# Four-layer graph stack: the layer normalisation moved from ScalarE to VectorE, its maximum taken in a later eviction, and ScalarE's order of work changed

## The reference, cut to what matters

```
h = max(layernorm(x), 0); x = x + gru_gnn(h, adj)       # layer 0: 5 message steps with a GRU cell
h = max(layernorm(x), 0); x = x + gated_gnn(h, adj)     # layer 1: gate, homophilic and heterophilic part, elu
h = max(layernorm(x), 0); x = x + grouped_gcn(h, adj)   # layer 2: 5 groups among nodes 0..24, two convolutions each
h = max(layernorm(x), 0); x = x + gcn(h, adj)           # layer 3
layernorm(x) = (x - mean) / sqrt(var + 1e-5), over the 128 features
```

## Time and profile before

| | us |
|---|---|
| median of 3 runs | 786.51 (783.95 to 788.78) |
| profiled execution | 786.21 |
| its span, first to last instruction | 784.4 |
| PE busy | 691.5 (88%) |
| DVE busy | 599.7 (76%) |
| ACT busy | 521.8 (67%) |
| POOL busy | 298.6 (38%) |

### The profile page before, as it was taken

One profiled execution on the slowest core, in us unless ns is written; L12 is line 12 of the kernel. 1 busy time (PEld: TensorE's weight loads), 2 busy tenths in 40 slices (PEclk: granted clock), 3 DMA queues, 4 the chain that ended last, 5 costly groups with the idle time before them and its releaser, 6 DMA issues.

```text
span 784.4 us, 12359 instructions
## 1 busy us (share of the span) xinstructions
PE 691.5 (88%) x4091; PEld 583.5 (74%) x4091; DVE 599.7 (76%) x1461; ACT 521.8 (67%) x1083; POOL 298.6 (38%) x423
## 2 busy tenths in 40 slices
PE   3899899989999979989999989989999989975765
PEld 2678588878888768878888767878788867865544
DVE  4688997888978966888978977888976877876143
ACT  5566677578778766668768757767767656646533
POOL 4222424573334343363343343463332242453320
PEclk9999989999999999999999999999999999999769
DMA  6600011100000020300000020210000000200001
GB/s 152 167 26 1 2 35 25 51 2 4 8 1 1 1 57 21 116 28 3 7 3 1 1 57 10 72 28 4 6 3 1 1 1 1 80 28 7 5 1 55
DMA packets 47623, 21.08 MB, mean 27 GB/s; under 512 B 9032, under 2 KB 47560, under 8 KB 47560
## 3 DMA queue, kind: packets, MB, share of 16 engines
q1 hardware_dynamic: 47560, 20.29, 9.6%
HBM read 15.27 MB, written 4.19 MB: 25 GB/s over the span
## 4 chain that ended last, share of the span: by engine, by line
PE 43%; DVE 30%; ACT 13%; POOL 8%; issue 5%; DMA 1%; DVEq 0%; SPq 0%; POOLq 0%; ACTq 0%
PE bank L404 7%; PE bank L405 7%; PE bank L406 6%; PE bank L399 5%; DVE zd L1292 4%; DVE hd L1304 4%; DVE h L1296 4%; DVE bank L1318 3%; DVE rh L1315 3%; POOL rstd L908 2%; PE bank L593 2%; ACT bank L880 2%; ACT xn L689 2%; PE bank L528 2%; DVE h_hi L1299 2%
## 5 line engine op out<-in xcount | busy, mean ns | idle before, releaser
L924 POOL TENSOR_TENSOR h_lo<-h,h_hi 128x512 fp32r<-128x512 f32 x64 | 81.8, 1279 | 339.8 <-DVE h_hi L1299 339.8
L404 PE MATMUL bank<-h_hi,whh_hi 128*128 128x512 f32 x240 | 106.7, 445 | 13.3 <-DVE rh L1315 12.8
L1315 DVE SCALAR_TENSOR_TENSOR rh<-bank,rh 128x512 f32<-128x512 f32 x80 | 55.0, 687 | 68.6 <-ACT bank L874 68.6
L404 PE MATMUL bank<-g_hi,wc_hi 128*128 128x512 f32 x240 | 103.6, 432 | 0.7 <-DVE h L1296 0.3
L406 PE MATMUL bank<-h_lo,whh_hi 128*128 128x512 f32 x240 | 96.3, 401 | 0.0
L405 PE MATMUL bank<-h_hi,whh_lo 128*128 128x512 f32 x240 | 96.1, 401 | 0.0
L405 PE MATMUL bank<-g_hi,wc_lo 128*128 128x512 f32 x240 | 94.9, 395 | 0.0
L406 PE MATMUL bank<-g_lo,wc_hi 128*128 128x512 f32 x240 | 94.8, 395 | 0.0
L399 PEld LDWEIGHTS bank<-edge,hn 128*128 128x128 f32 x640 | 83.6, 191 | 8.2 <-issue 1.0
L689 ACT ACTIVATE xn<-x_res,shift,rstd 128x128 f32<-128x128 f32 x128 | 55.8, 485 | 48.7 <-POOL shift L910 48.7
L399 PE MATMUL bank<-edge,hn 128*128 128x128 f32 x640 | 84.3, 274 | 0.8 <-ACT hn L859 0.8
(11 more groups left out here) (167 smaller groups left out, 1605.9 us busy)
## 6 DMA issues: line engine op xcount, KB each, us to landing
x_in<-in_x SPq DMA_DIRECT2D x8, 512.0 KB, 5.4
adj_in<-in_adj SPq DMA_DIRECT2D x8, 512.0 KB, 4.8
x_res<-in_x SPq DMA_DIRECT2D x16, 256.0 KB, 2.8
out_x<-x_res SPq DMA_DIRECT2D x16, 256.0 KB, 2.3
xz<-x_res SPq DMA_DIRECT2D x16, 50.0 KB
w_sb<-in_L_gnn_W SPq DMA_DIRECT2D x1, 640.0 KB, 5.1
w_sb<-in_L_gnn_W SPq DMA_DIRECT2D x5, 128.0 KB, 5.0
rows<-in_adj SPq DMA_DIRECT2D x32, 0.6 KB
```

The costliest lines, as they stand in the source:

```text
L404: nc.tensor.matmul(dst[:], w_hi, m_hi, start=start, stop=False)
L924: nc.gpsimd.tensor_tensor(h_lo[q][:], h[q][:], h_hi[q][:].bitcast(f32), ALU.subtract).then_inc(sem["h_lo_new"], 1)
L1315: nc.vector.scalar_tensor_tensor(rh[:], R_BANK[:], 1.0, rh[:], ALU.add, ALU.mult).then_inc(sem["rh_ready"], 1)
```

## The change

- **Normalisation.** ACT's `norm_relu` and `zone_norm` go. DVE gets `norm`, four `tensor_scalar` a quad, (x - mean) * rstd, both read per partition from tiles, at NORM1, NORM3 and NORM0, all four graphs in the first of the two slots, and `zone_norm` at NORM2. POOL's -mean and shift go, with one wait.
- **Maximum.** It is taken where the transpose is evicted (`first_h`, `read_zone`, `read_last_norm`: Copy becomes Relu). In layer 1, where xn is multiplied untransposed too, ACT does it in place, `second_norm`, one 128x512 activation a quad at NORM1 + 1 (slots -1, 1, 3, 5).
- **Second support.** `read_support2` moves from DVE to ACT, ahead of `read_hidden`.
- **Order on ACT.** `beside(2n+1)` no longer comes before the next step's eviction of H_BANK but behind it, ahead of `turned_h`; only `l1_read_linear` stays at the end of the step. `read_blocks` moves ahead of `second_norm`.
- **DVE's slots.** `make_bias_rows` goes from slot 20 to slot 8; the second half of `group_blocks` from slot 23 to slot 24.

The diff, with the declarations of tiles and semaphores left out:

```diff
...
 TURN_ADJ, DEGREES_ABS, DEGREES, GROUP_DEGREES, GROUP_BLOCKS, TURN_BLOCKS = 22, 12, 17, 20, 22, (27, 29)
-DEGREE_NORMS, ADD_IDENTITY, MASK_ROUND, LAST_NORMS, BIAS_ROWS = 26, 31, 34, 38, 24
+BIAS_AT = 8
+DEGREE_NORMS, ADD_IDENTITY, MASK_ROUND, LAST_NORMS = 26, 31, 34, 38
 STATS0, AGGR0, NORM0, TURN0, EDGES, SPLIT = 13, 14, 16, 26, 33, 35
...
         def _(act):
-            def norm_relu(L, r, q, src, dst, graphs=range(QUAD)):
-                i = 0 if L == 0 else 1
-                if graphs[0] == 0:
-                    act.wait_ge(sem[f"ln{L}_rstd"], r * QUADS + q + 1)
-                for j in graphs:
-                    b = q * QUAD + j
-                    last = nc.scalar.activation(dst[:, b, :], src[:, b, :], ACT.Relu,
-                                                bias=shift[i][:, b:b + 1], scale=rstd[i][:, b:b + 1])
-                if graphs[-1] == QUAD - 1:
-                    last.then_inc(sem[f"ln{L}_xn"], 1)
+            def second_norm(r, q):
+                act.wait_ge(sem["l1_centred"], r * QUADS + q + 1)
+                nc.scalar.activation(xn[:, cols(q), :], xn[:, cols(q), :], ACT.Relu).then_inc(sem["ln1_xn"], 1)
...
                     act.wait_ge(sem["h_new"], (r - 1) * STEPS + q + 1)
-                nc.scalar.activation(hx[q][:], (C_BANK if r else (A_BANK, B_BANK)[q % 2])[:], ACT.Copy
+                nc.scalar.activation(hx[q][:], (C_BANK if r else (A_BANK, B_BANK)[q % 2])[:], ACT.Relu
                                      ).then_inc(sem["hx_ready"], 1)
...
-            for q in range(QUADS):
-                norm_relu(0, 0, q, x_in, x_in)
             for q in range(QUADS):
...
-            def zone_norm(r, q):
-                act.wait_ge(sem["ln2_rstd"], r * QUADS + q + 1)
-                nc.scalar.activation(xz[0:PACKED, q, :], xz[0:PACKED, q, :], ACT.Relu,
-                                     bias=shift[2][0:PACKED, q:q + 1], scale=rstd[2][0:PACKED, q:q + 1]
-                                     ).then_inc(sem["ln2_xn"], 1)
             def read_zone(r, q):
                 act.wait_ge(sem["zone_turned"], r * QUADS + q + 1)
-                nc.scalar.activation(zone[:, q, :], H_BANK[:, 0:PACKED], ACT.Copy).then_inc(sem["zone_ready"], 1)
+                nc.scalar.activation(zone[:, q, :], H_BANK[:, 0:PACKED], ACT.Relu).then_inc(sem["zone_ready"], 1)
...
+            def read_support2(r, k):
+                n = TILES[k][3]
+                act.wait_ge(sem["l2_sup2"], r * NT + k + 1)
+                nc.scalar.activation(sup2[0:n, k % 2, :], C_BANK[0:n, 0:128], ACT.Copy).then_inc(sem["l2_sup2_read"], 1)
             def read_group(r, k, at):
...
                 act.wait_ge(sem["ln3_turned"], r * QUADS + q + 1)
-                nc.scalar.activation(hT[q % 2][:], quad(A_BANK[:, :]), ACT.Copy).then_inc(sem["ln3_h"], 1)
+                nc.scalar.activation(hT[q % 2][:], quad(A_BANK[:, :]), ACT.Relu).then_inc(sem["ln3_h"], 1)
...
                     l1_read_turned(r, q)
-                for r, q in due(slot, 1, LINEAR1):
-                    l1_read_linear(r, q)
                 for r, k, _ in second_conv(slot)[-1:]:
...
                     read_group(r, k, at)
+                for r, k in tile_at(slot, 2):
+                    read_support2(r, k)
                 for r, k in tile_at(slot, 1):
...
                     l1_exp(r, q)
-                for r, q in due(slot, 1, NORM2):
-                    zone_norm(r, q)
                 for r, _ in due(slot, 1, PACK_EARLY, units=1):
...
                 for half in range(2):
-                    for r, q in due(slot, 1, NORM1 + half):
-                        norm_relu(1, r, q, x_res, xn, range(2 * half, 2 * half + 2))
-                    for r, q in due(slot, 1, NORM3 + half):
-                        norm_relu(3, r, q, x_res, xn, range(2 * half, 2 * half + 2))
-                    for r, q in due(slot, -1, NORM0 + half):
-                        norm_relu(0, r, q, x_in, x_in, range(2 * half, 2 * half + 2))
+                    for r, _ in due(slot, 0, TURN_BLOCKS[half], units=1):
+                        read_blocks(r, half)
+                for r, q in due(slot, 1, NORM1 + 1):
+                    second_norm(r, q)
                 for r, q in due(slot, 0, TURN_ADJ, pace=1):
...
                     first_h(r, q)
-                for half in range(2):
-                    for r, _ in due(slot, 0, TURN_BLOCKS[half], units=1):
-                        read_blocks(r, half)
...
                 nc.scalar.activation(g_hi[:], TG[:], ACT.Copy).then_inc(sem["g_hi_ready"], 1)
+            def linear_beside(slot):
+                for r, q in due(slot, 1, LINEAR1):
+                    l1_read_linear(r, q)
...
                 nc.scalar.activation(rh[:], H_BANK[:], ACT.Identity, bias=bhh[:, 2:3]).then_inc(sem["hb_ready"], 1)
+                beside(2 * n - 1)
                 if n + 1 < ALL:
...
                 nc.scalar.activation(I_BANK[:], I_BANK[:], ACT.Tanh, bias=bih[:, 2:3]).then_inc(sem["n_ready"], 1)
-                beside(2 * n + 1)
+                linear_beside(2 * n + 1)
             for n in range(ALL, ALL + TAIL_STEPS):
+                beside(2 * n - 1)
                 beside(2 * n)
-                beside(2 * n + 1)
+                linear_beside(2 * n + 1)
+            beside(2 * (ALL + TAIL_STEPS) - 1)
...
             nc.gpsimd.memset(neg_half[:], -0.5)
-            nc.gpsimd.memset(neg_one[:], -1.0)
             nc.gpsimd.memset(eps_ln[:], LN_EPS)
...
                 pool.wait_ge(sem[f"ln{L}_mv"], r * QUADS + q + 1)
-                nc.gpsimd.tensor_tensor(var_eps[i][0:p, c], mv[i][0:p, c, 1], eps_ln[0:p, c], ALU.add)
-                nc.gpsimd.tensor_tensor(neg_mean[i][0:p, c], mv[i][0:p, c, 0], neg_one[0:p, c], ALU.mult).then_inc(sem[f"ln{L}_var"], 1)
+                nc.gpsimd.tensor_tensor(var_eps[i][0:p, c], mv[i][0:p, c, 1], eps_ln[0:p, c], ALU.add).then_inc(sem[f"ln{L}_var"], 1)
                 pool.wait_ge(sem[f"ln{L}_var"], r * QUADS + q + 1)
-                nc.gpsimd.tensor_tensor(rstd[i][0:p, c], var_eps[i][0:p, c], neg_half[0:p, c], ALU.pow).then_inc(sem[f"ln{L}_pow"], 1)
-                pool.wait_ge(sem[f"ln{L}_pow"], r * QUADS + q + 1)
-                nc.gpsimd.tensor_tensor(shift[i][0:p, c], neg_mean[i][0:p, c], rstd[i][0:p, c], ALU.mult).then_inc(sem[f"ln{L}_rstd"], 1)
+                nc.gpsimd.tensor_tensor(rstd[i][0:p, c], var_eps[i][0:p, c], neg_half[0:p, c], ALU.pow).then_inc(sem[f"ln{L}_rstd"], 1)
...
+            def norm(L, r, q, src, dst, done):
+                i = 0 if L == 0 else 1
+                dve.wait_ge(sem[f"ln{L}_rstd"], r * QUADS + q + 1)
+                for j in range(QUAD):
+                    b = q * QUAD + j
+                    last = nc.vector.tensor_scalar(dst[:, b, :], src[:, b, :], mv[i][:, b, 0:1], rstd[i][:, b:b + 1],
+                                                   ALU.subtract, ALU.mult)
+                last.then_inc(sem[done], 1)
+            def zone_norm(r, q):
+                dve.wait_ge(sem["ln2_rstd"], r * QUADS + q + 1)
+                nc.vector.tensor_scalar(xz[0:PACKED, q, :], xz[0:PACKED, q, :], mv[2][0:PACKED, q, 0:1],
+                                        rstd[2][0:PACKED, q:q + 1], ALU.subtract, ALU.mult).then_inc(sem["ln2_xn"], 1)
             def edges(r, q):
...
                 mean_variance(0, 0, q)
+            for q in range(QUADS):
+                norm(0, 0, q, x_in, x_in, "ln0_xn")
             dve.wait_ge(sem["weights_loaded"], 16 * N_EARLY)
...
-            def read_support2(r, k):
-                n = TILES[k][3]
-                dve.wait_ge(sem["l2_sup2"], r * NT + k + 1)
-                nc.vector.tensor_copy(sup2[0:n, k % 2, :], C_BANK[0:n, 0:128]).then_inc(sem["l2_sup2_read"], 1)
             def add_group(r, k):
...
                     mean_variance(1, r, q)
+                for r, q in due(slot, 1, NORM1):
+                    norm(1, r, q, x_res, xn, "l1_centred")
+                for r, q in due(slot, 1, NORM3):
+                    norm(3, r, q, x_res, xn, "ln3_xn")
+                for r, q in due(slot, -1, NORM0):
+                    norm(0, r, q, x_in, x_in, "ln0_xn")
+                for r, q in due(slot, 1, NORM2):
+                    zone_norm(r, q)
                 for r, q in due(slot, 1, STATS2):
...
                     l1_gate(r, q)
-                for r, k in tile_at(slot, 2):
-                    read_support2(r, k)
                 for r, k, _ in second_conv(slot):
...
                     degrees(r, q)
-                if slot == BIAS_ROWS - 4:
+                if slot == BIAS_AT:
                     make_bias_rows()
...
                     group_degrees(r)
-                for r, half in due(slot, 0, GROUP_BLOCKS, pace=1, units=2):
+                for r, half in due(slot, 0, GROUP_BLOCKS, pace=2, units=2):
                     if half == 0:
...
```

(9 more changed lines are left out.)

## The result

The kernel after takes 820.85 us (median of 4 runs, 818.99 to 822.00) against 785.37 us before on the same chip: ratio 1.0399, 95% interval 1.0359 to 1.0440. The forecast was 776.2. The sign was wrong.

The account below looks back on a forecast made before the run. PE was taken as the bound in most slots, DVE close, with ACT's in-order queue carrying POOL's delay into PE in slots 26 to 31. Three rounds -10.8, first round +2.3, start and tail -1.5: 786.2 becomes 776.2 us, range 760 to 793.

Parts of the forecast that it names:

- Slots 26 to 31 (-5.5 a round): Three rounds: ACT no longer delays the norm, rh and PE's turn come earlier, eviction waits go; -5.5 us a round, bounds -8, -2.
- the eviction's wait (3.2 a round): Slots 26 to 31: PE's wait for H_BANK's eviction, 9.5 us over 11 waits, 3.2 a round, all goes.
- rival B: The eviction's wait only changes its name, as ACT's moved work stands ahead of turned_h: 791.5 us; chance 0.17.
- Slot 32 (+2.2): Fourth quad's norm on DVE is held by four POOL operations ahead of rh: +2.2 us a round, bounds 0 and +3.6.
- Slot 38 and slots 0 to 6 (+1.8 and +1.2): NORM1's first quad held by POOL, +1.8 us a round; ACT's fuller queue in slots 4 and 6 and DVE's order, +1.2.
- Slots 8 to 25 (-3.3): PE's waits for eviction and second support go, layer 0's norm costs about 0.3: -3.3 us a round, bounds -4, +2.
- Four instructions in 0.65 us: DVE's price for one quad's four norm tensor_scalar in a row: 0.65 us, between 0.45 and 1.1.
- First round (+2.3): DVE-bound slots 16 to 23 take four norms, bias rows move from slot 20 to 8: +2.3 us, bounds -1.5, +5.
- Start and tail (-1.5): Shorter instructions at the start, a shorter first norm of layer 3 in the tail: -1.5 us together, bounds -5, +2.
- A: Collisions of DVE's norms with POOL cost nothing, as short instructions slip in between: 762.4 us; chance 0.26.
- C: DVE becomes the bound in slots 36 to 2 and 16 to 22, norms held at nearly every quad: 807 us; chance 0.13.
- slots 26 to 31 no shorter than 30 us a round: Sign named ahead that the forecast is wrong: slots 26 to 31 still take 30 us a round or more.

Follow-up runs that it names:

- e3: The kernel after with VectorE's norms of layers 1, 3 and 0 listed behind the other work of their slot: 802.80 us, ratio 1.0164.
- e1: The kernel before with only two ScalarE parts: H_BANK's eviction ahead of the work beside, second support copied by ScalarE: 785.23 us, ratio 0.9958.
- e2: The kernel after with ScalarE's old order and the second support copied by VectorE again: 824.70 us, ratio 1.0442.
- e5: e3's kernel with GpSimd's add_identity in slots 32 and 38 waiting until the norm beside it is done: 787.09 us, ratio 0.9971.
- e14: Zone's norm added on VectorE to a kernel with the ScalarE parts and only layer 3's norm there (757.66 us): 764.33 us, ratio 0.9680.
- e13: Layer 0's norm of rounds 1 to 3 added on VectorE to a kernel with ScalarE's parts and only layer 3's norm there (757.66 us): 770.09 us, ratio 0.9751.

## Why the forecast was wrong, by its own steps

- **Slots 26 to 31 (-5.5 a round)** is the step that failed. With slot 32 it holds 22 of the 46 us between the forecast and the trace; 11 lie in start and tail, 10 in slots 8 to 25. The step let four norm instructions end 0.65 us after rstd and rh follow. The listing of `beside` puts the norms ahead of zone_residual and its statistics, so rstd is waited for with nothing in between (2.36 us), and 1.11 + 0.67 + 0.87 us come behind it before rh. With slot 32 the forecast had -3.3; measured were +2.9, +3.7 and +5.9. e3 moves nothing but this order and gives 18 us back.
- In the same step, **the eviction's wait (3.2 a round)** was counted as won. e1 shows that it isn't: PE's wait at L562 goes, and the steps of slots 24 to 34 stay as long. After against e2 says the same with the norm on VectorE. That rh sets their length instead is a reading: PE's wait for rh rose from 12.8 to 16.9 us in e1. This was rival B's case, in these slots alone, and not by B's mechanism, which wanted a new wait of PE there.
- **Slot 32 (+2.2)**: the collision is there, but it takes 3.5 a round (e5), near the upper bound of 3.6. The forecast gave 2 us of slack away because rh had been idle 2.83 us; that idle time was itself the wait for ScalarE, and the change had removed it (in e3 VectorE waits 0.39 us there, for rstd).
- **Slot 38 and slots 0 to 6 (+1.8 and +1.2)**: together +3.0 forecast, +3.1, +3.4 and +3.0 measured. The sum is right, partly by luck: slots 36 and 38 alone gave about +1 a round (the held norm +4, less 3.2 for ScalarE's wait that went, which the forecast didn't count), and slots 0 to 6 about +2.2, most of it in slot 4.
- **Slots 8 to 25 (-3.3)**: measured about -0.1 in slots 8 to 22. ScalarE's part was right (-3.5 in e1). Missing were the prices of the zone's norm, taken as nothing (+2.1 to +2.5 a round there in e14), and of layer 0's, taken as 0.3 a round (+2.9 in two of the rounds in e13, where it stands behind the other work): two of its four quads collide (1.51 and 1.71 us instead of 1.11; 1.98 each in e13).
- **Four instructions in 0.65 us**: 1.11, the upper bound. The overlap of the neighbours in the earlier trace rows was taken for their pitch.
- **First round (+2.3)**: +4.3 up to slot 34, within its bounds; bias rows cost 2.0 in slots 8 and 10 instead of 0.9, and layer 0's norm 3.9 (e13).
- **Start and tail (-1.5)**: +3.8, and +5.9 with the last step. In the tail the order costs again (3.8, e3), and one quad of the zone shows the worst hold of all, in the timeline of POOL, DVE and PE:

```profile
764.60 4.03 POOL L949 TENSOR_TENSOR adjTI<-adjTI,dis 128x512 f32<-128x512 f32 x4
764.67 4.04 DVE L1016 TENSOR_SCALAR xz<-xz,mv,rstd 100x128 f32<-100x128 f32 x1 [0.93 <-POOL rstd L896]
...
768.86 0.40 PE L504 MATMUL bank<-ident,xz 100*128 100x100 f32 x1 [2.64 <-DVE xz L1016]
```

The rivals: A (collisions cost nothing) fell, they cost 12 us by the spans of e3 and e5 and 16 by the medians. C came nearest in its time (807) and has a part of the mechanism. Its first sign showed: in the steps of slots 36 to 2 VectorE is busy for 92% of the time, 87% before (windows of before and after, DVE the third busy time):

```profile
328.59:366.92 38.33, 36.01 (x231) 31.19 (x230) 33.49 (x88) 26.36 (x51) 21.41 (x27) 1.00 0.08 23
342.27:381.77 39.50, 35.53 (x219) 31.13 (x218) 36.22 (x102) 23.61 (x39) 19.17 (x19) 0.96 0.07 21
```

Its second didn't: PE waits for rh there once, 3.1 us in slot 38, not all through; and the norms are held at four quads of twelve. The largest loss lies in slots 26 to 32, where VectorE is at 70 to 85%: there it stood waiting or was held, and a full queue was not the bound. Of the other signs named ahead, "slots 26 to 31 no shorter than 30 us a round" showed, but says little: these steps took 31.7 us in each round, and 31.4, 29.9 and 30.0 before. Most signs of being right showed too (no wait left for the eviction or the support, 23.9 us behind the first tanh, over 1 us for some norms in slots 32 and 38); they name waits that go, and the time went the other way.

## What to carry to other kernels

Work that is moved to another in-order queue takes its wait with it: read where in the new engine's list it lands, and what stands behind it, before counting the wait as gone. Move it only for those pieces whose old wait set the end (here layer 3: 22 us won, while the other layers cost 25), and let work that is ready stand ahead of the wait. In this kernel a `tensor_scalar` on SBUF beside GpSimd's large operations took as long as those operations did, and the cheap cure was to let GpSimd wait, as it was busy for only 34% of the span. And a trace counts each wait once: that one is gone says nothing of the time until the step's own length is measured (e1).
